# Ring sizes of two adjacency streams in a graph-attention layer: mask 3 to 2, plain sums 3 to 4

## What is computed

```python
type_sum_a = adj_a @ x                       # "plain sums", also used for adj_b @ x
attn_a = sigmoid(concat([type_sum_a, x]) @ Wa.T + ba)
attn_b = sigmoid(concat([type_sum_b, x]) @ Wb.T + bb)
h = x @ W_sa
scores = s_left[:, None] + s_right[None, :]  # two dots of h with a_sa
e = where(adj_a != 0, exp(-leaky_relu(scores, 0.01)), 0.0)
x_a = (e / (sum(e, axis=1) + 1e-05)) @ h
x_b = adj_b @ (x @ W_gcnb) + b_gcnb
out = layernorm(x + sigmoid(attn_a * x_a + attn_b * x_b))
```

## Time and profile before

| what | value |
|---|---|
| median of three runs | 944.23 us |
| profiled execution, its own time | 943.85 us |
| span in the profile, first to last instruction | 942.0 us |
| time outside the span | 1.85 us |
| TensorE (PE) busy | 931.0 us, 99% of the span |
| VectorE (DVE) busy | 684.7 us, 73% |
| ScalarE (ACT) busy | 357.0 us, 38% |
| GpSimd (POOL) busy | 204.5 us, 22% |
| DMA traffic | 121.06 MB, mean 129 GB/s |

### The profile page before, as it was taken

The page is one execution under the profiler, slowest core; times in us unless marked ns, Lnnn a source line. Parts: engine busy times, 40 slices in busy tenths (PEclk is TensorE's granted clock), DMA queues, the critical chain, the costliest instruction groups (busy, mean ns, idle before and its releaser), DMA issues.

```text
span 942.0 us, 12638 instructions
## 1 busy us (share of the span) xinstructions
PE 931.0 (99%) x4276; PEld 774.1 (82%) x4276; DVE 684.7 (73%) x1285; ACT 357.0 (38%) x618; POOL 204.5 (22%) x508
## 2 busy tenths in 40 slices
PE   9999999999999999999999999999999999999996
PEld 6888878888888888888888888888888888898885
DVE  5999968976677676677676677587587576576757
ACT  4554545433333342343242343343343332343312
POOL 2111100321321221321221321221221221222142
PEclk9999999999999999999999999999999999999998
DMA  9779754346444446444446444546444536444431
GB/s 268 185 181 228 193 147 107 101 120 132 119 123 116 129 119 124 122 125 117 127 114 129 126 115 117 132 110 129 130 112 118 134 107 107 117 124 101 118 73 46
DMA packets 191441, 121.06 MB, mean 129 GB/s; under 512 B 59280, under 2 KB 162576, under 8 KB 191376
## 3 DMA queue, kind: packets, MB, share of 16 engines
q1 hardware_dynamic: 102720, 62.42, 22.6%
q0 software_dynamic: 35904, 44.31, 21.9%
q10 hardware_dynamic: 52752, 13.51, 7.3%
HBM read 107.35 MB, written 12.86 MB: 128 GB/s over the span
## 4 chain that ended last, share of the span: by engine, by line
PE 96%; DMA 1%; issue 1%; DVE 1%; ACT 1%; SPq 0%; POOLq 0%; POOL 0%; DVEq 0%; ACTq 0%
PE bank L605 16%; PE bank L607 16%; PE bank L606 16%; PE bank L631 14%; PE bank L630 14%; PE bank L654 5%; PE bank L655 5%; PE bank L656 5%; PE bank L616 2%; PE bank L617 2%; PE bank L588 1%; DMA w_gate<-w_sa_t_dram 1%; DMA adj_r<-adj_t_dram 0%; PE bank L642 0%; ACT u L393 0%
## 5 line engine op out<-in xcount | busy, mean ns | idle before, releaser
L605 PE MATMUL bank<-e_hi,x_hi 128*128 128x512 f32 (+1 forms) x728 | 272.9, 375 | 0.8 <-DVE e_lo L780 0.8
L607 PE MATMUL bank<-e_lo,x_hi 128*128 128x512 f32 (+1 forms) x728 | 272.3, 374 | 0.0
L606 PE MATMUL bank<-e_hi,x_lo 128*128 128x512 f32 (+1 forms) x728 | 272.2, 374 | 0.0
L401 ACT ACTIVATE e_hi<-u,c_col 128x512 fp32r<-128x512 f32 (+1 forms) x182 | 126.1, 693 | 329.7 <-DVE u L771 222.6
L352 POOL DMA_DIRECT2D adj_r<-adj_t_dram x180 | 104.4, 580 | 647.7 <-PE bank L631 538.9
L630 PE MATMUL bank<-x_hi,adj_r 128*128 128x512 f32 x572 | 222.8, 389 | 0.0
L631 PE MATMUL bank<-x_lo,adj_r 128*128 128x512 f32 x572 | 222.7, 389 | 0.0
L780 DVE SCALAR_TENSOR_TENSOR e_lo<-u,c_col,e_hi 128x512 fp32r<-128x512 f32 (+1 forms) x182 | 129.9, 714 | 44.8 <-ACT e_hi L401 35.2
L605 PEld LDWEIGHTS bank<-e_hi,x_hi 128*128 128x128 f32 x728 | 137.0, 188 | 26.3 <-issue 1.2
L606 PEld LDWEIGHTS bank<-e_hi,x_lo 128*128 128x128 f32 x728 | 137.0, 188 | 25.0
L607 PEld LDWEIGHTS bank<-e_lo,x_hi 128*128 128x128 f32 x728 | 137.0, 188 | 24.5
(11 more groups left out here) (122 smaller groups left out, 835.2 us busy)
## 6 DMA issues: line engine op xcount, KB each, us to landing
adj_r<-adj_t_dram POOLq DMA_DIRECT2D x158, 256.0 KB, 3.2
adj<-adj_t_dram SPq DMA_DIRECT2D x156, 256.0 KB, 3.1
out_dram<-y SPq DMA_DIRECT2D x24, 256.0 KB, 3.8
z_blocks<-z2s ACTq DMA_DIRECT2D x23, 256.0 KB, 2.5
z2t<-z_blocks ACTq DMA_DIRECT2D x92, 64.0 KB, 3.0
z1s<-x_dram SPq DMA_DIRECT2D x14, 256.0 KB, 6.1
adj<-adj_t_dram SPq DMA_DIRECT2D x26, 128.0 KB, 2.3
adj_r<-adj_t_dram POOLq DMA_DIRECT2D x22, 128.0 KB, 2.3
```

The source lines that it names most:

```text
L401: nc.scalar.activation(e_hi[g % E_RING][:, 0:cols(b)], u[g % U_RING][:, 0:cols(b)], ACT.Copy, scale=c_col[:, j:j + 1]).then_inc(e_hi_ready, 1)
L605: nc.tensor.matmul(z1[k][:, 0:n], x_hi[:, j, kk], e_hi[s][:, 0:n], start=(j == 0), stop=False)
L606: nc.tensor.matmul(z1[k][:, 0:n], x_lo[:, j, kk], e_hi[s][:, 0:n], start=False, stop=False)
L607: ins = nc.tensor.matmul(z1[k][:, 0:n], x_hi[:, j, kk], e_lo[s][:, 0:n], start=False, stop=(j == TILES - 1))
```

## The change

The mask ring goes from three buffers to two, the ring of the plain sums from three to four; the total of 256 KB buffers stays six. The early load of the third mask tile goes, since there is no third buffer to load ahead.

```diff
-ADJ_RING = 3
-ADJ_R_RING = 3
+ADJ_RING = 2
+ADJ_R_RING = 4
...
             load_piece(6)
-            load_adj(2)
             load_piece(7)
             for j in range(TILES):
                 if j + STAGES < PIECES:
                     load_piece(j + STAGES)
                 load_adj(j + ADJ_RING)
```

## The result

The changed kernel takes 946.63 us, the median of 11 runs (943.22 to 949.56). The kernel before took 944.19 beside it (11 runs, 943.35 to 945.57). The ratio is 1.0027 [1.0019, 1.0034]: slower by 0.27%, 2.4 us, where 0.5 us were forecast. The time also scatters over 6.3 us, where that of the kernel before scatters over 2.2.

The account below looks back on a forecast made before the run. PE was taken as the bound, busy 931.0 of 942.0 us. -0.53 at the head and +0.6 at step 10 vanish in the wait at 133.85, ending 0.45 later: 944.3, or 944.7 against the median; range 943.3 to 946.6.

Parts of the forecast that it names:

- The head: Near 19 us, the fourth plain-sum buffer removes PE's wait for a tile: a gain of 0.53 us.
- Step 10 behind the store: Block 0: the mask tile issued at 53.43 behind the `l_rows` store comes 5.0 us late; PE waits 0.6.
- The chain to PE: End of block 0: DVE's 3.4 us pass through weight piece, `l_row` and `u`; PE resumes 0.45 us later.
- the tile of step 13 in time: Block 0, behind the gate vectors: lands at 73.6, wanted at 74.7, a microsecond to spare.
- rival 2: Step 13's tile also late, landing at 79.2: DVE loses 4.5 us more, 948.8 in profile's terms; chance 0.16.
- what a wait of PE costs: Step 10 and start of block 1: PE waits counted at their length, 0.6 us and 0.45 us later.
- Rival 1: Step 10's tile lands by 63.4, PE never waits there, head's 0.53 stays: 943.3 in profile's terms; chance 0.22.

Follow-up runs that it names:

- changed_2: The changed kernel without further edit, run again on the third chip; 945.67 us, 1.0019 of the kernel before.
- again: The changed kernel without further edit, run on the first chip for a second trace; 948.96 us, 1.0036 of the kernel before.
- gates_early_2: The changed kernel with the four gate transfers behind step 4 instead of step 10, on the third chip; 943.40 us, 0.9993 of the kernel before.
- gates_early: The changed kernel with the four gate transfers behind step 4 instead of step 10, on the second chip; 943.71 us, 0.9994 of the kernel before.
- after_flat: The changed kernel with row l stored as 16 contiguous bytes a partition, output not the reference's; 943.50 us, 0.9991 of the kernel before.
- before_again: The kernel before, unedited, one run for a trace on the second chip; 944.33 us.
- split_store: The changed kernel with the row l store cut into four stores of 128 elements, behind steps 4 to 7; 953.23 us, 1.0070 of the kernel before.

## Why the prediction was off

It gave 944.7 and no measurable change; it is 946.63, just beyond the 946.6 that ended its range, and 0.27% is clear of no change by its interval. Put by its own steps:

- **The head: right.** The wait near 19 us is gone in each trace of the changed kernel. From PE's first plain-sum row to its first `sum_z1` are 11.14 us before (10.91 to 11.27 in the other traces of that kernel and its variants) and 10.69, 10.45 and 10.69 in the three traces of the changed kernel: 0.45 to 0.69 for the 0.53 forecast.
- **Step 10 behind the store: right in kind and place.** DVE waits 3.3, 4.0 and 5.0 us for its tile in the three traces, forecast 5.0. But it was argued that the landing repeats because the places ahead of it are the same to the microsecond. They are, and the store isn't: 8.6, 9.4 and 10.0 us here, 8.6 to 13.5 over all single-element whole stores traced behind step 7. In the three traces DVE's lateness grows with the store's time; that this is the scatter of all executions is inferred.
- **The chain to PE: right.** DVE, last weight piece, `l_row`, `u` of step 26, PE. The three traces of the changed kernel, against the kernel before (us; minus is earlier):

| trace | DVE late at step 13 | `u` of step 26 | PE resumes | extra in step 26 | sum | measured |
|---|---|---|---|---|---|---|
| first | 2.27 | -0.12 | -0.66 | 0 | -0.66 | -0.63 |
| `changed_2` | 3.60 | +0.87 | +0.32 | 1.32 | 1.64 | 1.82 |
| `again` | 5.60 | +3.84 | +3.30 | 1.57 | 4.87 | 4.83 |

  The working said that 3.4 us of DVE bring 0.9 at `u` and 0.45 at PE; the row with 3.60 has 0.87 and 0.32. From 3.60 to 5.60 PE's lateness grows by 2.98 for 2.00, since the weight piece is 2.2 us later and the `l_row` took 5.8 us instead of 5.0.
- **Failed: the tile of step 13 in time, "a microsecond to spare".** This was the step at which the forecast and rival 2 parted, and rival 2 was given 0.16. The tile was issued at 69.14 in `again`, where 69.6 was assumed, but it landed 7.7 us later, not 4.0. The 1.75 MB counted ahead of it were too little: in the stretch from 69.1 to 76.9 the core moved 274 GB/s, 2.1 MB, and the backlog was not gone at 68. DVE's wait at step 13 is 0.8 to 1.6 us, with the tile there at 76.9 in `again` and not at 79.2: milder than rival 2's sum. With the gate vectors elsewhere the tile took 3.0 and 3.9 us, behind them 6.8 to 7.7, so what is queued ahead, and not the bytes of the tile, sets it. The Trainium skill, DMA: Bandwidth & Descriptors, anatomy of one DMA, gives a fit for transfers that GpSimd issues, by which 256 KB would take an estimated 2.6 us; these tiles are issued by SP, and only the undisturbed 3.0 comes near it.
- **Failed: what a wait of PE costs.** The sum took PE's wait at its length. In two of the three traces the clock fell behind it and added 1.3 to 1.6 us in step 26; counted to the third matmul of step 27 it is 1.57 and 1.58, and in the traced execution of `changed_2` that is most of the loss. The prediction had no such term. How often it counts, the mean granted clocks on record tell in part: 0.996 or less came only in traces with a fall, 0.998 only in those without. Of the eleven executions of the changed kernel in the result the six slowest, from the median up, have 0.995 or 0.996; two of the five faster have 0.998 and took 945.22 and 946.04, so 1.0 and 1.9 us were lost without a fall.
- **The rivals.** Rival 1 gave 943.3 in the profile's terms with both the gain and an early `l_row`; the first trace, at 943.22, is that case, reached with the store at its shortest. Rival 2 described the others in kind. That `again`, at 948.68, is so near its 948.8 is luck: PE resumed 3.30 us late, not 4.9, and the clock, which rival 2 didn't have, added 1.57.

Shown by taking each away: with one late tile left, the loss is gone (`gates_early_2` beside `changed_2`, `gates_early`, `after_flat`). In the traces the loss goes with how late DVE is at step 13 in all: 1.3, 2.0 and 1.6 us in these three and 2.27 in the first trace, where both tiles were late, cost nothing; 3.60 and 5.60 did. In the two traces with early gate vectors the store took 8.6 and 9.3 us; on the first chip, where whole stores took 10.0 to 13.5 in the traces, this kernel was not run, so whether the tile of step 10 alone can cost time there is open.

Not settled: why a store of 128 elements took about as long as one of 512, why stores differ from execution to execution, and which waits bring the clock down. Nor why the kernel before itself took 946.58 on the first chip: its mean granted clock was 0.996 or less in 9 of 29 executions there, in none of 27 on the second chip and one of 33 on the third, and `before_again`, meant to trace such an execution, came out at 944.33. That the other executions behind the median of 946.63 lost their time in the same two ways is inferred from three traces.

## What to carry to other kernels

The median landing of 3.1 us didn't tell whether two buffers are enough here; the places at 9.4 to 11.0 and 6.8 to 7.7 did. To size a ring, list what stands ahead of each load in the queue, and look at two or three executions of any odd store before trusting its one duration. When a load becomes late, follow the issuing queue past it: what was issued behind it (here 1 MB of gate vectors) slides into the next tile's time, and two stalls that each fit the slack need not fit it together. Here moving the bulk transfer did what the third buffer had done.

## What the runs showed of the chip

- A 2 KB store in 4-byte elements took 8.6 to 13.5 us behind step 7 and 8.2 to 12.1 in the later blocks; a quarter of one, alone on its way, 9.0; in 16-byte pieces 3.1 and 4.2 behind step 7, up to 4.8 later. What is issued behind it waits: the next mask tile took 9.4 to 11.0 us in the three traces of the changed kernel. So does a tile on another queue: GpSimd's, issued half a microsecond behind the store, took 11.7, 12.5 and 13.4 us in these traces. The Trainium skill, DMA: Bandwidth & Descriptors, Specifications, wants 512 B for full rate. The direction agrees.
- PE's granted clock fell to 0.50, its 1.2 GHz level, for 3.41 us behind or shortly after PE waits of 1.82, 1.88, 2.19 and 3.12 us, and did not behind waits of 1.15, 1.47, 2.44 (`split_store`, 139.04) and 2.64 us. A wait's length alone doesn't tell it. Each of the two falls that were counted cost 1.6 us.
